# Other orders of work within the rounds of three software pipelines in a graph network kernel on Trainium2

## The reference

```python
x = _layernorm(x + _L0_gnn_ref(x, W_neigh, b_neigh, src, dst))      # mean of neighbours, concat, @ W
x = _layernorm(x + _L1_gnn_ref(x, edge_index, W1, W2))              # two GCN2 layers
x = _layernorm(x + _L2_gnn_ref(x, edge_index, edge_attr_16, ...))   # GATv2, norm, gelu feed-forward, norm
x = _layernorm(x + _L3_gnn_ref(x, ..., src, dst))                   # two GAT layers
```

## Time and profile before

| what | value |
|---|---|
| median of 3 runs | 7529.38 us |
| profiled execution, its own time | 7521.0 us |
| its span | 7519.1 us |
| mean granted TensorE clock | 0.769 of full |
| PE / DVE / ACT / POOL busy | 53% / 44% / 30% / 49% |
| n0: blocks start from 1097.0 to 1534.4 us | 98 |
| n1: from about 2800 to 3118 us | 98 |
| n2: from about 4464 to 5370 us | 98 |

### The profile page before, as it was taken

The page is one execution under the profiler, slowest core; times in us unless marked ns, Lnnn a source line. Parts: engine busy times, 40 slices in busy tenths (PEclk is TensorE's granted clock), DMA queues, the critical chain, the costliest instruction groups (busy, mean ns, idle before and its releaser), DMA issues. The chain is left out here.

```text
span 7519.1 us, 103124 instructions
## 1 busy us (share of the span) xinstructions
PE 3962.8 (53%) x21453; PEld 2742.6 (36%) x21454; DVE 3333.9 (44%) x13934; ACT 2255.2 (30%) x6392; POOL 3670.1 (49%) x4923
## 2 busy tenths in 40 slices
PE   4421667733641667456666858888502069602068
PEld 3311656622641655323332226656301057501023
DVE  4310235511210238534456647776505268605368
ACT  0000336511420446422222226666300034300035
POOL 3655015564036004344442547776672745572778
PEclk7555889965875889878888879999755589855589
DMA  1011225523432447541110013333322179622179
GB/s 22 1 46 54 71 93 180 177 79 84 141 106 60 140 141 252 173 157 33 34 30 12 28 48 118 114 119 115 92 59 66 39 239 291 201 61 67 40 251 312
DMA packets 551030, 816.76 MB, mean 109 GB/s; under 512 B 118566, under 2 KB 267629, under 8 KB 550466
## 3 DMA queue, kind: packets, MB, share of 16 engines
q1 hardware_dynamic: 354484, 506.90, 22.3%
q10 hardware_dynamic: 127152, 184.90, 6.6%
q0 software_dynamic: 69184, 122.90, 6.5%
HBM read 493.48 MB, written 329.46 MB: 109 GB/s over the span
## 5 line engine op out<-in xcount | busy, mean ns | idle before, releaser
L619 POOL DMA_INDIRECT agg_dst<-e_rows,e_put_i x392 | 404.5, 1032 | 392.0 <-DVEq L646 273.2
L931 PE MATMUL e1a_bank<-y_rows,e1a_hot 128*128 x1584 | 277.4, 334 | 345.2 <-issue 251.8
L1861 POOL DMA_INDIRECT e_rows<-h,e_other_i x392 | 383.8, 979 | 150.2 <-issue 118.9
L931 PE MATMUL e_bank<-x_rows,e_hot 128*128 x1584 | 274.7, 332 | 344.8 <-issue 239.5
L931 PE MATMUL e1b_bank<-y_rows,e1b_hot 128*128 x1584 | 273.5, 331 | 346.4 <-issue 257.7
L892 POOL DMA_INDIRECT y_rows<-m,s_other_i x196 | 187.7, 958 | 437.9 <-POOLq L101 377.7
L1701 PE MATMUL lg_z_ps<-gat_wl,lg_tr 128*128 128x512 f32 x392 | 246.8, 715 | 275.9 <-DVE lg_at L1757 127.8
L931 PEld LDWEIGHTS e1a_bank<-y_rows,e1a_hot 128*128 128x128 f32 x1584 | 253.0, 235 | 369.9 <-issue 369.4
L931 PEld LDWEIGHTS e_bank<-x_rows,e_hot 128*128 128x128 f32 x1584 | 251.1, 232 | 368.6 <-issue 368.2
L931 PEld LDWEIGHTS e1b_bank<-y_rows,e1b_hot 128*128 128x128 f32 x1584 | 249.7, 232 | 370.3 <-issue 369.7
L1472 POOL TENSOR_TENSOR n_rstd<-n_mv,minus_half 128x4 f32<-128x4 f32 x98 | 104.7, 1069 | 538.3 <-DVE n_mv L1565 538.3
(11 more groups left out here) (511 smaller groups left out, 12267.7 us busy)
## 6 DMA issues: line engine op xcount, KB each, us to landing
n_ag<-agg_dst SPq DMA_DIRECT2D x294, 264.0 KB, 3.9
n_xs<-x SPq DMA_DIRECT2D x294, 256.0 KB, 3.5
h<-n_ho ACTq DMA_DIRECT2D x196, 264.0 KB, 3.4
n_hs<-h SPq DMA_DIRECT2D x196, 264.0 KB
agg_dst<-e_ev SPq DMA_DIRECT2D x196, 132.0 KB
y<-n_o ACTq DMA_DIRECT2D x98, 264.0 KB, 3.7
e1a_fed<-y SPq DMA_DIRECT2D x196, 132.0 KB
m<-e1a_ev SPq DMA_DIRECT2D x196, 132.0 KB
```

The source lines that it names most:

```text
L619: pool.indirect_dma_start(out=agg, out_offset=bass.IndirectOffsetOnAxis(ap=e.put_i[:, c:c + 1], axis=0), in_=rows[:, c, :], in_offset=None ...
L931: ins = pe.matmul(bank[:, bass.ds(to * 512 + h * width, summed)], hot[:, s, k, h * P:(h + 1) * P], rows[:, bass.ds(chunk, 1), 0:summed], s ...
L1861: pool.indirect_dma_start(out=rows[:, c, :], out_offset=None, in_=h, in_offset=bass.IndirectOffsetOnAxis(ap=e.other_i[:, c:c + 1], axis=0))\
```

## The change

Only the lists given to `pipeline` change: the lags, and the order within a round. No instruction is added or removed in a block's work.

```diff
 # n0, node_sage
-                pipeline(pool, (0, degree), (3, deviation), (3, factor))
+                pipeline(pool, (0, degree), (4, deviation), (4, factor))
-                pipeline(pe, (2, product), (1, turn_over))
+                pipeline(pe, (2, turn_over), (3, product))
-                pipeline(act, (4, apply), (1, move), (4, store))
+                pipeline(act, (2, move), (5, apply), (5, store))
-                pipeline(dve, (0, mean), (3, sums))
+                pipeline(dve, (1, mean), (4, sums))
 # n1, node_gcn
-                pipeline(pe, (2, product), (1, turn_over))
+                pipeline(pe, (1, turn_over), (2, product))
-                pipeline(act, (5, store), (4, apply), (1, move))
+                pipeline(act, (5, store), (1, move), (4, apply))
-                pipeline(dve, (3, sums), (0, mix))
+                pipeline(dve, (0, mix), (3, sums))
 # n2, node_gatv2
-                pipeline(pe, (2, ffn1), (6, turn3), (3, ffn2), (7, product3), (1, turn1))
+                pipeline(pe, (2, turn1), (6, turn3), (3, ffn2), (7, product3), (2, ffn1))
-                pipeline(act, (8, store_h), (2, gelu), (5, third_norm), (5, store_x3), (1, first_norm), (6, move3), (7, keep_h),
-                         (1, move1))
+                pipeline(act, (8, store_h), (3, gelu), (2, move1), (5, third_norm), (5, store_x3), (6, move3), (1, first_norm),
+                         (7, keep_h))
```

## The result

The changed kernel took 7332.24 us in the median (7322.79 to 7338.43, 4 runs), the kernel before 7527.74 us beside it (7518.4 to 7531.32, 4 runs). The ratio is 0.9741, with a 95% interval of [0.9724, 0.9758]: 195 us faster. The forecast was 7309 us with a range of 7265 to 7400. The profiled execution took 7322.79 us, its span was 7320.9 us.

The account below looks back on a forecast made before the run. Loops of engines waiting for each other were taken to bound each stage. Gains of 111 (n0), 37 (n1) and 77 us (n2) make 225, 220 kept: 7521.0 becomes 7301, plus 8 for the median 7309; range 7265 to 7400.

Parts of the forecast that it names:

- its own sign: n0: the prediction calls itself wrong if ACT waits for anything but its own store; forecast round 3.36 us.
- the gap: ACT: idle from a norm's end to the next instruction, with the store directly behind that norm; 0.62 us.
- both loops: n0 before: DVE with POOL, and PE with ACT, wait for each other in loops both near 4.5 us.
- the load chain: n1: load, mix and sums must fit in three rounds, giving 2.65 to 2.83 us a round; 2.80 taken.
- the `gelu`'s chain: n2 before: gelu, third_norm, first_norm, turn1, move1, ffn1 and gelu again through ACT and PE; 8.94 us a round.
- The loop over two rounds: n2 after: longest loop, through gelu, ffn2, DVE's statistics, POOL's shift, ACT's norms and stores; 16.30 us, half 8.15.
- The 0.08: n2: added to 8.15 us for the loop's branch in each sixth round, giving 8.23.
- The bound of 8.6: n2: upper end of the round in us, if POOL's three deviations move against DVE's work and last longer.
- A: Rival, chance 0.17: n1's load chain decides (3.33 us a round), POOL's shift comes late in n2 (8.6); 7392 us.
- C: Rival, chance 0.04: ACT's stores directly behind their norms cost more than 0.62 us each; slower, 7636 us at 1.8 each.
- D: Rival, chance 0.03: the change does nothing, as another loop of the same length stands behind those that open; 7529 us.
- B: Rival, chance 0.10: ACT's stores cost nothing, issued while the datapath works; n0 3.23, n1 2.71, total 7221 us.

Follow-up runs that it names:

- e1: Kernel before with only n0's lists changed, n1 and n2 left as before: 6122.12 us, ratio 0.9827 to the kernel before.
- e5: Kernel before with only n0's new PE and ACT lists: 6232.94 us, ratio 1.0 to the kernel before.
- e6: Kernel before with only n0's new DVE and POOL lists: 6225.85 us, ratio 0.9988 to the kernel before.
- e4: Changed kernel with ACT's stores moved behind other queued work in all three stages: 5897.93 us, ratio 0.9467 to the kernel before.
- e7: Changed kernel with n1's DVE list as before (sums ahead of mix): 6014.97 us, ratio 0.965 to the kernel before.
- e11: Changed kernel with n2's bias product issued five times instead of once, ahead of the wait for the gelu: 7288.89 us, ratio 0.9692 to the kernel before.
- e8: Changed kernel with only n2's store_h moved, to behind move1: 7223.58 us, ratio 0.96 to the kernel before.
- e9: Changed kernel with only n2's store_x3 moved, to behind first_norm: 7263.46 us, ratio 0.9651 to the kernel before.

## Why the prediction was right, and the term that was off

**n0** came as forecast, 3.35 for 3.36. The prediction put it on ACT alone, and by its own sign, ACT waiting for anything but its store, it was wrong there: in 72 of 90 waits the trace names PE's transposes. PE's work and ACT's with the gap are both near 3.3 us. e1 shows the same round alone, e5 and e6 that both loops had to open, and e4 that 0.16 of the round is the store.

**n1** was 2.76 for 2.80. The forecast held that the load chain, DVE (2.71) and ACT (2.70) all end near each other. e7 shows that DVE's own work is 2.64, 0.07 less than the earlier trace rows gave (DVE's neighbours overlap more without the wait), and that the load adds 0.14 us a round. So the load chain was put at 2.80 in every round, while the trace shows DVE's work with a late load in some rounds; the total agrees in part by luck. The Trainium skill's rule on one transfer, in "DMA: Bandwidth & Descriptors", section "Anatomy of one DMA", is given there for a DMA that GpSimd issues, while these loads are issued by SP. The 3.2 us estimated from it do not fit them: a load issued at 2801.91 is wanted by the `mix` at 2806.86, 4.95 us later, and with that much in hand it still came late in 21 of some 88 rounds (in 12 of 87 in the first trace).

**n2** is the step that failed: "The rounds seen before were 8.94 us long in the steady part (the `gelu`'s chain) and 9.02 in the mean, since each sixth has the loop's branch; so 8.23". The loop over two rounds was right, 8.14 measured for 8.15. The 0.08 laid on it was not: 0.52 came (8.66 - 8.14), and the 0.43 between 8.66 and 8.23 are the 42 us by which n2's gain fell short. The 0.08 was read as the loop's branch, but the kernel before shows a fall of the clock in each of those rounds (L2178, 3.23 us instead of 1.98), and the same number of falls could not be counted on once PE's waits had moved. The change gathers PE's waits into one hole before each `ffn2`, 0.7 to 2.1 us in the rows above, and the granted clock now falls more often, in a part of `ffn2` (the round of 9.05, with 9.22 behind it) or in all of it (10.7). The time at 0.50 is some 107 us, for 58 before. e11 fills that hole and e8 shortens it by other means; both bring the clock back, e11 to 0.98 with rounds of 8.03, e8 to 1.00. The three executions with the same n2 show the price, half of the time at 0.50: 53 us of the stage, near the 0.52 a round (50 us). That the gathered hole is what brings more falls is supported by e8, e9 and e11, but why the clock falls in one round and not in another isn't shown. The bound of 8.6 was named for another mechanism, POOL's deviations lasting longer, and this was not what happened.

**The rest.** 11 us came outside the rounds counted, where nothing was forecast, and they hide a part of n2's shortfall in the total: 7332 for 7309 is closer than n2 alone (35 us for 77) would have it.

**The rivals.** A did not come: the load costs 0.14 us, not 0.5. C did not: the gap stayed at 0.62 to 0.71 us in all three stages. The POOL part of A, a late shift, was seen, but only behind a fall of the clock. D holds for each half of n0 alone. B is wrong for this kernel, in which ACT is idle behind each store, and right for e4, in which the same stores are issued over queued work.

What stays open is why e11 keeps 11 rounds at the lower clock, and how the falls start: PE was not idle for longer in the rounds before them than in others in which the clock stayed.

## What to carry to other kernels

When two loops of nearly the same length close over four engines, open both: n0's halves gave 0 and 6 us, together 109. An engine's DMA issue that waits for the engine's own last result stops everything behind it (0.62 us each, 1.13 for two); put it behind one piece of other queued work and it costs nothing. And when a reorder leaves TensorE a hole in every round, look at the granted clock in that stage before counting the round: here the lower clock cost 0.5 us a round more than the chain of waits said. A round of odd length in the trace before deserves the same look: here it was a fall of the clock and not the loop.

## What the runs showed of the hardware

TensorE's clock was worth more than a part of TensorE's work. Four added products of 512 columns in each block came with a kernel faster by 43 us, some 31 of them by the clock. Four products of `ffn2` take 0.61 us at a granted clock of 1.00 and 1.06 at 0.50, and the falls came in a stage where PE is busy for 84% of the time (703.86 of 839.70 us). The kernel before fell less with PE busy for 82% (680.22 of 830 us).

The 0.62 us behind a store is no property of the issue, which is 0.34 to 0.38 us long in the rows. The issue waits for the result, and the next activation waits for the issue: 1.13 us behind `store_h` in the changed kernel, nothing in e8 with the same two issues over a running `gelu`.
